# Three reciprocal roots move from GpSimd to VectorE, and twenty-eight scatters stand in one row

## The reference, cut to what matters

```
# last layer, attention: every block is read with channels as rows, 8 heads of 16 channels
qk  = einsum('bhdq,bhdl->bhql', qh, kh) / sqrt(16);  ret = einsum('bhql,bhdl->bhdq', softmax(qk), vh)
x   = x + g_xattn[3] * gamma * ret
# last layer, mixture: h is x under its layer norm, (x - mean) / sqrt(var + 1e-5)
scores = sigmoid(h @ gate_weight.T)
# four groups of four experts: the two best groups, in them the four best experts, weights normalized times 2.5
y = sum over the four chosen experts of w * (silu(h @ g.T) * (h @ u.T)) @ d.T, and a shared expert beside it
```

## Time and profile before

| | us |
|---|---|
| median of 3 runs (lowest to highest) | 1311.75 (1310.72 to 1312.32) |
| the profiled execution, its own time | 1311.41 |
| its span | 1309.6 |
| TensorE busy | 1094.1 (84%) |
| VectorE busy | 761.7 (58%) |
| GpSimd busy | 579.9 (44%) |
| ScalarE busy | 494.0 (38%) |
| channel heads end, mixture begins | about 1096 from the span's start |
| routed tiles of the last layer | 1136 to about 1270 |

### The profile page before, as it was taken

How to read it: one execution, slowest core, us unless ns; L and a number is a source line. 1 busy time by engine, 2 the same in 40 slices (tenths; PEclk the granted TensorE clock), 3 DMA queues, 4 the chain that set the end, 5 groups by cost and what they waited for, 6 DMA issues and landing times. The chain is left out here.

```text
span 1309.6 us, 25520 instructions
## 1 busy us (share of the span) xinstructions
PE 1094.1 (84%) x7222; PEld 802.4 (61%) x7223; DVE 761.7 (58%) x2784; ACT 494.0 (38%) x1309; POOL 579.9 (44%) x916
## 2 busy tenths in 40 slices
PE   4568899999999973999997999958887885799980
PEld 4345688877777751566655766634554544588860
DVE  6768344244444434687754555467878845555547
ACT  0046221223333320566663234415664532244430
POOL 5551027713333343555561524443332556455550
PEclk9998699999999995899998999968997966899995
DMA  9788962213333327111010334340000612366638
GB/s 402 205 261 280 340 214 107 107 51 109 107 106 106 107 89 308 50 65 51 2 42 18 108 87 132 117 153 1 2 2 2 251 71 83 112 161 165 163 118 321
DMA packets 92301, 169.45 MB, mean 129 GB/s; under 512 B 11102, under 2 KB 70750, under 8 KB 91230
## 3 DMA queue, kind: packets, MB, share of 16 engines
q1 hardware_dynamic: 72393, 107.63, 26.8%
q0 software_dynamic: 17664, 48.91, 10.3%
q10 hardware_dynamic: 2160, 11.86, 2.2%
HBM read 82.75 MB, written 85.61 MB: 129 GB/s over the span
## 5 line engine op out<-in xcount | busy, mean ns | idle before, releaser
L2152 PE MATMUL bank<-weights,xT 128*128 x832 | 241.9, 414 | 0.3 <-ACT xT L2246 0.2
L1974 POOL DMA_INDIRECT slots_out<-weights,y_rows x128 | 122.7, 959 | 136.2 <-DVE y_rows L2418 96.8
L2152 PEld LDWEIGHTS bank<-weights,xT 128*128 128x128 f32 x832 | 143.3, 192 | 24.8 <-issue 0.7
L1968 POOL DMA_INDIRECT slots_in<-xn_wide,row_in x110 | 106.2, 966 | 107.1 <-DMA slots_in<-xs_wide 50.5
L1974 POOL DMA_INDIRECT slots_out<-pack,y_rows x80 | 76.7, 959 | 144.7 <-DVE y_rows L2418 137.2
L2246 ACT COPY xT<-bank 128x256 f32<-128x256 f32 x208 | 77.4, 372 | 118.2 <-PE bank L2144 117.8
L2063 PE MATMUL bank<-xT,weights 128*128 128x256 f32 x416 | 106.7, 402 | 2.3 <-ACT xT L2210 2.3
L1408 PE MATMUL bank<-ctx,weights 32*128 32x256 f32 x512 | 80.9, 457 | 31.9 <-DVE weights L1559 25.9
L1481 ACT ACTIVATE weights<-bank 128x512 f32<-128x512 f32 x128 | 72.6, 596 | 72.2 <-PE bank L1416 72.2
L2395 DVE TENSOR_TENSOR weights<-weights,bank 128x128 f32<-128x128 f32 x128 | 36.8, 287 | 104.3 <-ACT weights L2250 104.3
L2063 PEld LDWEIGHTS bank<-xT,weights 128*128 128x128 f32 x416 | 81.7, 201 | 18.0 <-ACT xT L2210 4.1
(11 more groups left out here) (422 smaller groups left out, 2450.5 us busy)
## 6 DMA issues: line engine op xcount, KB each, us to landing
slots_in<-xs_wide SPq DMA_DIRECT2D x16, 2112.0 KB, 19.0
weights<-slots_in SPq DMA_DIRECT2D x96, 132.0 KB, 2.3
xs_wide<-slots_in SPq DMA_DIRECT2D x72, 132.0 KB, 2.3
weights<-slots_out SPq DMA_DIRECT2D x17, 512.0 KB, 9.2
rows<-slots_out SPq DMA_DIRECT2D x16, 512.0 KB, 3.3
weights<-in_l_gu SPq DMA_DIRECT2D x1, 7040.0 KB
pack<-slots_in SPq DMA_DIRECT2D x40, 132.0 KB, 2.1
weights<-in_l_gu ACTq DMA_DIRECT2D x1, 4608.0 KB, 14.2
```

Source lines behind the costliest of these rows:

```text
L1968: pool.indirect_dma_start(out=slots_in, in_=xn_wide[:, t, :], in_offset=None, out_offset=bass.IndirectOffsetOnAxis(ap=row_in[:, t, i:i + 1 ...
L1974: pool.indirect_dma_start(out=slots_out, in_=y[:, n % U, :], in_offset=None, out_offset=bass.IndirectOffsetOnAxis(ap=y_rows[:, n % U:n % U ...
L2152: last = nc.tensor.matmul(out, xT[:, n.c % 2, c, :], flat(gu_w[:, ds(e, 1), c, :]), start=(c == 0), stop=(c == C - 1 and layer != 2))
```

## The change: three roots, and the table of scatters

The roots of blocks 13, 14 and 15 leave GpSimd's list. VectorE computes them by a first guess from the bits of the number and three Newton steps, in ten small instructions, right behind the `vv` of that block. The table of scatters becomes 6, 6 and 28 at `b` = 13, 14, 15 (40 in all), and the mixture issues 24 in place of 28.

```diff
-            scatter_in = {13: 6, 14: 6, 15: 14, 16: 6, 17: 4}
+            scatter_in = {13: 6, 14: 6, 15: 28}
+            guess = carve([P, 2])
+            OWN_ROOTS = 13
...
-                    if there(b - 3):
+                    if there(b - 3) and b - 3 < OWN_ROOTS:
                         roots(b - 3)
...
-                        act.wait_ge(rooted, b - 1)
+                        if b - 2 < OWN_ROOTS:
+                            act.wait_ge(rooted, b - 1)
+                        else:
+                            act.wait_ge(late_rooted, 2 * (b - 2 - OWN_ROOTS + 1))
...
+                late_step = Chain(dve, late_own)
+                def own_root(r):
+                    v, y, a = vv[:, r % 2, :], guess[:, 0:1], guess[:, 1:2]
+                    dve.wait_ge(var_ready, r + 1)
+                    dve.wait_ge(r_normed, r - 1)
+                    late_step(nc.vector.tensor_scalar(a.bitcast(I32), v.bitcast(I32), 1, None, ALU.logical_shift_right))
+                    late_step(nc.vector.tensor_scalar(y.bitcast(I32), a.bitcast(I32), -1.0, float(0x5f3759df), ALU.mult,
+                                                      ALU.add))
+                    for three in (3.0, 12.0, 768.0):
+                        late_step(nc.vector.scalar_tensor_tensor(a, y, v, y, ALU.mult, ALU.mult))
+                        late_step(nc.vector.scalar_tensor_tensor(y, a, three, y, ALU.subtract, ALU.mult))
+                    nc.vector.tensor_scalar(rr[:, r % 2, :], y, -1.0 / 8192, None, ALU.mult).then_inc(late_rooted, 1)
+                    nc.vector.tensor_scalar(off[:, r % 2, :], mv[:, r, 0:1], y, 1.0 / 8192, ALU.mult, ALU.mult
+                                            ).then_inc(late_rooted, 1)
...
-                            dve.wait_ge(rooted, b - 3)
+                            dve.wait_ge(rooted, min(b - 3, OWN_ROOTS))
                         nc.vector.tensor_scalar(vv[:, b % 2, :], mv[:, b - 2, 1:2], LN_EPS, None, ALU.add
                                                 ).then_inc(var_ready, 1)
+                        if b - 2 >= OWN_ROOTS:
+                            own_root(b - 2)
...
-            mixture(3, rt, carve, LAST, scattered, 12)
+            mixture(3, rt, carve, LAST, scattered, 8)
```

More of the change, by code:

```diff
@@ L1169, in channel_heads @@
              rooted, r_normed, r_turned, rx_ready, l_ready, l_taken, tri_ready, marked, sel_ready, counted, cnt_copied,
-             route_own, placed, pool_own, padded, c_turned, c_copied, bias_ready, b_added, joined, head_var) = (
+             route_own, placed, pool_own, padded, c_turned, c_copied, bias_ready, b_added, joined, head_var, late_own,
+             late_rooted) = (
                 sem(n) for n in ("f", "normed", "k", "v", "s", "m", "mt", "xm", "st", "e", "pv", "pvc", "ot", "i", "o",
@@ L1173, in channel_heads @@
                                  "rx", "l", "ltaken", "tri", "marked", "sel", "counted", "cntc", "rown", "placed",
-                                 "pown", "padded", "ct", "cc", "bias", "ba", "joined", "hvar"))
+                                 "pown", "padded", "ct", "cc", "bias", "ba", "joined", "hvar", "lown",
+                                 "lrooted"))
             loads = ((0, 2), (2, 6), (6, 11), (11, NB))
```

## The result

The changed kernel takes 1306.1 us in the median of 11 runs (1302.94 to 1310.21), the kernel before 1311.68 in 11 (1306.54 to 1313.82). The ratio is 0.9966, 95% interval 0.9953 to 0.9979: by the ratio 4.5 us faster (2.8 to 6.2), while the two medians lie 5.6 apart. I had forecast 1310.2, 1.6 us faster, with a range of 1308.4 to 1312.3. The sign was right, the size was not.

A forecast was written before the change was run, and what follows sets the result against it. The end of GpSimd's row of scatters was taken to set when TensorE's last routed tiles begin. Scatters 1.09 and clock 0.5 gave 1.6 us less: 1309.8 for the profiled execution, 1310.2 for a median, range 1308.4 to 1312.3.

The forecast's parts named there:

- The end of GpSimd's row sets the start of the tiles: Last layer: TensorE's routed tiles wait 6.27 us for a load issued 2.05 us after GpSimd's last scatter ends.
- The chain costs 2.1 us ahead of the placing, that of block 13 nothing: VectorE, heads: block 14's ten-instruction root delays placing of blocks 7 to 11 by 2.1 us; block 13's fills idle time.
- GpSimd reaches the barrier when its last scatter has ended, so the mixture begins 2.13 us late: Barrier between heads and mixture: GpSimd arrives last, at 1097.65 against 1095.52, so the mixture begins 2.13 us later.
- A new wait of 2 us ahead of block 12: Mixture: GpSimd's ninth scatter waits about 2 us for the later placing, in place of the four scatters removed.
- Scatters 1.09 us less: GpSimd's row: the last sixteen scatters start at 1110.76, not 1111.85, so their end moves 1.09 us earlier.
- Clock 0.5: Routed tiles: a TensorE pause of 3.05 us, not 6.27, shortens the time at half clock; gain 0.5 us.
- Second rival, second chunk at half clock: Mixture's start: shared expert's second chunk at half clock makes placing 1.76 us late; 0.7 us slower, 1312.4; chance 0.1.
- Third rival, VectorE's chain holds up scatters: Heads: chain dearer, or block 15's holds back GpSimd by 2.1 us; total 1312.2 or 1312.8; chance 0.06.

The follow-up runs named there:

- place_first: Changed kernel, but VectorE computes block 14's root behind the placing of blocks 7 to 11, not ahead of it; ratio 0.9956 to the kernel before.
- longer_15: Changed kernel with eight more dependent instructions, result unused, in block 15's chain on VectorE; ratio 0.9962 to the kernel before.
- all_48: Changed kernel, but 36 scatters at `b` = 15 in place of 28, leaving 16 in the mixture; ratio 0.9972 to the kernel before.
- old_table: Changed kernel with its roots on VectorE, but the table of scatters as before the change (28 in the mixture); ratio 0.9977 to the kernel before.
- before_warm10: Kernel before the change with ten unused multiplications in TensorE's pause ahead of the routed tiles; ratio 0.9990 to the kernel before.
- after_again: The changed kernel itself, unaltered, run and profiled once more; median 1306.95 us.
- only_15: Kernel before with only block 15's root moved to VectorE, blocks 13 and 14 on GpSimd, old scatter table; ratio 0.9984 to the kernel before.
- pf_warm3: place_first with three unused multiplications in TensorE's pause ahead of the routed tiles; median 1304.2 us, ratio 0.9949 to the kernel before.

## Why the prediction was wrong

- *The end of GpSimd's row sets the start of the tiles*: right. In the two profiles compared first, the first tile moved by 3.78 us and the row's end by 3.81. In place_first the row moved by 2.06 more and the first tile by 2.05; in longer_15 a later mixture moved neither.
- *The chain costs 2.1 us ahead of the placing, that of block 13 nothing*: right, 2.03, and block 13's falls into idle time (ScalarE's `xn` of block 13 starts at 18.3 of the row's time, 18.6 before).
- *GpSimd reaches the barrier when its last scatter has ended, so the mixture begins 2.13 us late*: this step failed, and the size with it. GpSimd's sequencer had passed the barrier with scatters still queued (three in the changed kernel, eleven in all_48), so it opened when ScalarE, the last of the others, had ended, and the mixture began 2.6 us early. I had forecast that end rightly and then thrown it away for GpSimd's. I took the time a scatter occupies GpSimd for the time its sequencer needs. The earlier trace rows could have raised the question, since "POOLq" there names the sequencer apart from the engine's own work; they don't answer it, because GpSimd was out of work at that barrier.
- *A new wait of 2 us ahead of block 12*: followed from that step and fell with it. In the first profile there was none (placing over at 54.04, due at 56.7), in the second one of 0.74, through the clock.
- *Scatters 1.09 us less*: it was 3.81. The missing 2.7 us stand in my own sum: a break of 0.7 us at the barrier (the mixture's first scatter at 1098.65, where the pitch made it due at 1097.95) and the wait of 2.0 us ahead of block 12. Both followed from the failed step, and neither came. By the runs the roots' move takes 2.73 of the 3.81 (old_table), and the 28 in a row behind it the other 0.8 to 1.1; in the other order the shares may differ.
- *Clock 0.5*: undersized. In the two profiles of the changed kernel, gains of 3.81 and 3.51 in the row became 5.24 and 5.14 at the fifth tile, so 1.4 to 1.6. My reason for it failed as well: the pause was not the 3.05 us that I had worked out but 5.36 and 2.79, the clock was at half when the tiles began both times, and the gain came from an earlier rise, which no run ties to the change. By these runs it is partly luck: place_first lost 1.0 of its 2.06 to the clock, and all_48, 3.51 ahead of the kernel before in the row, is 3.45 ahead at the fifth tile and so gained nothing. The bounds (nothing to 2 us) were fair for the changed kernel; for the whole price of the slow start before_warm10 shows 2.8 where I had said 2.
- *Second rival, second chunk at half clock*: it happens (after_again, old_table, all_48) and in after_again moves placing by 2.7 us, more than the 1.76 I had given it, but it does not end slower, since the mixture starts early.
- *Third rival, VectorE's chain holds up scatters*: no. Twelve scatters beside block 15's chain and all else keep their pitch (from 1080.95 to 1094.86, 1.265 each), so the rule of the Trainium skill that I had weighed (DMA: Bandwidth & Descriptors, SWDGE vs HWDGE vs iDMA) has no visible effect here. The page ties the lock to one mode of VectorE (the 2-port perf mode), and no row tells whether these instructions ran in it.

That scatters queued ahead carry the row across the barrier is shown by all_48 and old_table. In the kernel before nothing was queued there. GpSimd's last scatter and root of the heads:

```profile
1090.45 0.96 POOL L1295 DMA_INDIRECT slots_in<-xn_wide,row_in  x1 [0.30 <-issue]
...
1092.11 0.26 POOL L1289 TENSOR_SCALAR rows<-rows 128x1 f32<-128x1 f32 x1
```

Its scatters were over at 1091.41 and block 15's root at 1092.37, and ScalarE ended the heads only at 1095.52. So the break of 4.15 us there is of the same kind as the 4.33 of only_15, where block 15's root was gone: the time from GpSimd's last work to late heads. Whether that root, whose steps wait for VectorE, would also keep the sequencer from running ahead was not tried.

## What to carry to other kernels

In these runs a row of DMAs on an engine spans a barrier without a gap when enough of them are queued ahead of it to last until the other engines have arrived, and nothing behind them on that engine has to wait. So put the issues ahead of the barrier, and move small work that other engines wait for off the issuing engine: behind a row of scatters it comes late, and the stage ends late with it. Ask of a barrier when an engine's sequencer reaches it, not when its last work ends. Put what a long row waits for (here the placing) ahead of what a short chain can afford to get later: exchanging two neighbours was worth 2 us of the row.

## What the runs showed of the hardware that I had not expected

- GpSimd's sequencer passed a barrier with at least eleven indirect DMAs not yet started (all_48), and in the changed kernel, with three, the row kept its 1.265 us pitch across it.
- TensorE's clock changes are not tied to a place in the work: in two profiles of the same program it rose at 47.0 and at 53.7 of the row's time at the mixture's start. After the restart at the tiles it rose 6.5 us later in the kernel before and in all_48, 3.6 and 3.2 in the changed kernel. It fell in place_first's pause of 3.34 us, and stayed at 2.4 GHz where three multiplications stood in that pause (pf_warm3).
